# Half of a dense expert stage moved into a state-space recurrence, with B and C read from a ring of half-size tiles

## What is computed

```
h = adapter + layernorm(x)                       # per sequence, by language
for l in range(4):                               # the recurrence: 4 Mamba layers
    xz = norm(h) @ W_in;  u = silu(conv4(xs)+cb);  z = ...
    dt, B, C = split(u @ W_x);  dt = softplus(dt @ W_dt + b)
    for t: s = exp(dt*A)*s + dt*u*B ;  y = sum_states(s*C)      # 256 channels, 16 states
    h = h + ((y + u*Dp) * silu(z)) @ W_out
x1 = x + h
y = sum_e w_e * (silu(x1@Wg_e) * (x1@Wu_e)) @ Wd_e   # dense stage: 8 experts and a shared one, F = 512
out = x1 + top2_moe(y)                               # routing and sparse stage: 8 experts, gelu
```

## Time and profile before

| | |
|---|---|
| median of 3 runs | 2935.45 us (2935.06 to 2936.15) |
| profiled execution, its own time | 2935.85 us |
| its span, first to last instruction | 2934.1 us |
| VectorE busy / TensorE busy / GpSimd busy / ScalarE busy | 72% / 86% / 61% / 50% |
| mean granted TensorE clock | 0.946 |
| memory traffic | 354 MB, mean 121 GB/s |

### The profile page before, as it was taken

The page is one execution under the profiler, slowest core; times in us unless marked ns, Lnnn a source line. Parts: engine busy times, 40 slices in busy tenths (PEclk is TensorE's granted clock), DMA queues, the critical chain, the costliest instruction groups (busy, mean ns, idle before and its releaser), DMA issues. The chain is left out here.

```text
span 2934.1 us, 27727 instructions
## 1 busy us (share of the span) xinstructions
PE 2515.8 (86%) x6470; PEld 1112.9 (38%) x6470; DVE 2104.9 (72%) x2075; ACT 1456.5 (50%) x2337; POOL 1780.1 (61%) x1090
## 2 busy tenths in 40 slices
PE   5588888888888888888888888869999999999586
PEld 3233333333333333333333333324444444444264
DVE  4399999999999999999999999972333333333221
ACT  2366657666666665666566667632222222222222
POOL 3278887888888788888888887861022202221266
PEclk9798999999999999989999999999999999999798
DMA  7334533543453344345434533516000000000154
GB/s 204 139 128 179 201 127 144 194 170 127 170 197 139 136 185 186 127 157 196 154 128 174 205 127 142 195 61 220 8 15 8 15 7 11 25 8 1 45 111 70
DMA packets 130514, 354.33 MB, mean 121 GB/s; under 512 B 21716, under 2 KB 85410, under 8 KB 97570
## 3 DMA queue, kind: packets, MB, share of 16 engines
q1 hardware_dynamic: 116770, 342.46, 32.1%
q0 software_dynamic: 11264, 7.98, 1.8%
q10 hardware_dynamic: 2432, 3.38, 0.3%
HBM read 330.34 MB, written 23.99 MB: 121 GB/s over the span
## 5 line engine op out<-in xcount | busy, mean ns | idle before, releaser
L683 POOL TENSOR_TENSOR gg<-hh,Ct 128x1024 f32<-128x1024 f32 x512 | 1205.0, 2356 | 336.2 <-DVE hh L598 322.4
L598 DVE TENSOR_TENSOR_SCAN hh<-dA,psdB 128x1024 f32<-128x1024 f32 x512 | 1170.7, 2287 | 59.4 <-ACT dA L543 6.1
L385 PE MATMUL psY<-gg,ident 128*128 128x512 f32 x2048 | 1024.4, 636 | 128.0 <-POOL gg L683 127.7
L543 ACT ACTIVATE dA<-dt,Acur 128x508 f32<-128x508 f32 x1024 | 664.6, 707 | 14.9 <-DVE hh L598 14.4
L385 PEld LDWEIGHTS psY<-gg,ident 128*128 128x128 f32 x2048 | 390.9, 200 | 689.8 <-issue 420.6
L592 DVE TENSOR_TENSOR psdB<-psU,Bt 128x1024 f32<-128x1024 f32 x512 | 617.6, 1206 | 36.8 <-ACT psU L522 36.8
L1051 DVE TENSOR_TENSOR ac<-sg,d_bank 128x512 f32<-128x512 f32 x288 | 198.1, 688 | 514.0 <-PE d_bank L901 496.8
L948 ACT ACTIVATE sg<-d_bank 128x512 f32<-128x512 f32 x288 | 171.9, 597 | 534.6 <-PE d_bank L897 521.3
L811 POOL TENSOR_TENSOR xw<-x1T,wbc 128x512 f32<-128x512 f32 x72 | 74.9, 1041 | 568.1 <-PE d_bank L901 563.8
L897 PE MATMUL d_bank<-x1T,wgu 128*128 128x512 f32 x576 | 296.6, 597 | 1.9 <-DMA wgu<-in_Wu 1.9
L901 PE MATMUL d_bank<-xw,wgu 128*128 128x512 f32 x576 | 295.5, 595 | 0.0
(11 more groups left out here) (149 smaller groups left out, 1887.1 us busy)
## 6 DMA issues: line engine op xcount, KB each, us to landing
Bt<-rows SPq DMA_DIRECT2D x128, 1024.0 KB, 6.0
Ct<-rows SPq DMA_DIRECT2D x128, 1024.0 KB, 4.7
wcur<-taps_l SPq DMA_DIRECT2D x33, 512.0 KB
disp<-zrow SPq DMA_DIRECT2D x16, 528.0 KB, 12.1
dx<-disp SPq DMA_DIRECT2D x16, 528.0 KB, 6.5
wcur<-in_W_inT SPq DMA_DIRECT2D x33, 128.0 KB
diag<-diags_l SPq DMA_DIRECT2D x33, 128.0 KB
ad_gb<-in_gb SPq DMA_DIRECT2D x32, 128.0 KB, 3.3
```

The lines of the kernel that those rows point to most:

```text
L385: ins = pe.matmul(psY[:, :], lhsT=ident[:, :], rhs=gg[k % NGB][:, j, :], start=False, stop=(k % NK == NK - 1 and j == 1))
L543: ins = act.activation(dA[k % NDA][:, j, :, 1:T], dt[p][:, c, :, 1:T], ACT.Exp, scale=Acur[p][:, s:s + 1])
L598: dve.tensor_tensor_scan(out=hh[k % NHB][:, :, :].rearrange("p c t -> p (c t)"), data0=dA[k % NDA][:, :, :, :].rearrange("p c q t -> p (c ...
L683: pool.tensor_tensor(gg[k % NGB][:, :, :], hh[k % NHB][:, :, :], Ct[:, s:s + 2, :], ALU.mult).then_inc(prod, 1)
```

## The change

1. **Order of the recurrence.** The 32 iterations are 4 layers of groups 0 to 3, and after them 4 layers of groups 4 to 7 (`layer`, `group`; `ROUND` = 4). All is unrolled, no loop is left in the recurrence or the dense stage.
2. **Dense stage of groups 0 to 3 inside the second half** (iterations from `FIRST` = 15). Nine rounds per iteration are threaded through the steps by `G_AT`, `U_AT`, `D_AT`: gate, up and down products on TensorE, a copy of each gate out of PSUM (`place_gate`), one silu over the nine (`silu_gates`) beside the iteration's own, one product each on VectorE (`act_product`), the scaling on GpSimd (`scale`). Weights come from memory once for each group. The dense stage that follows has four groups.
3. **PSUM.** One of the two `psdB` tiles becomes the gate and up tiles, one of the two tiles for `dt*u` the down sum. So from iteration 13 (`RING0`) there is one `psdB` and one `psT`, filled for each channel half just before it (`turn0`, `turn1`).
4. **SBUF.** From iteration 13, B and C are rings of four pairs each; the second channel half takes the pairs backwards, 7 to 0. There are 12 loads of one pair of B and one of C for each iteration, 512 KB each.
5. **Steps by halves.** From iteration 15, in 8 of 16 steps (`PAIRED`) GpSimd adds the two halves of `gg`, and TensorE does one product instead of two.
6. **Given steps.** In iterations 0 to 12, GpSimd makes the input term of three steps (`GIVEN`) in SBUF, and ScalarE moves it into `psdB`.
7. The residual is added by one more identity product in the output projection, and no longer by GpSimd. The dispatch buffer is cleared during the recurrence. `x0` stands on TensorE ahead of the step 0 sums.

```diff
-NCK, CKS = 4, NS // 4
-WUSE = 9
-OUTP = 7
+ROUND = NG // 2
+NPR = NS // 4
...
+FIRST = NL * ROUND - 1
+RING0 = FIRST - 2
...
-ACT_AT = {1: ["params", "dtu1"], 2: ["norm"], 3: ["sums1"], 5: ["x0"], 6: ["x1"], 7: ["z0", "z1"], 8: ["silu"], 10: ["bcdt"], 11: ["dt0", "dt1"],
+ACT_AT = {1: ["params", "dtu1"], 2: ["turn0", "norm"], 3: ["sums1"], 5: ["x0"], 6: ["x1"], 7: ["z0", "z1"], 8: ["silu"], 10: ["turn1", "bcdt"], 11: ["dt0", "dt1"],
...
+GIVEN = {4: 0, 9: 5, 13: 8}
+POOL_AT = {3: ["gate1"], 6: ["rstd"], 10: ["dt"], 11: ["dtu"], 12: ["gate0"]}
+G_AT = [-9, -8, -6, -5, -4, -3, -2, -1, 3]
+U_AT = [6, 8, 9, 11, 12, 14, 15, 19, 20]
+D_AT = [10, 10, 11, 13, 14, 18, 18, 21, 22]
+T_AT = 5
+PAIRED = [0, 1, 2, 5, 8, 13, 14, 15]
...
+def pair(i, k):
+
+    return k if k < NK else (k - NK if i < RING0 else NSTEP - 1 - k)
...
+                    last = 1 if i >= FIRST and k in PAIRED else 2
+                    for j in range(last):
+                        ins = pe.matmul(psY[:, :], lhsT=ident[:, :], rhs=gg[k % NGB][:, j, :], start=False, stop=(k % NK == NK - 1 and j == last - 1))
...
+                def silu_gates(v):
+                    act.wait_ge(gfree, use_g(NB * v + NB - 1) + 1)
+                    lo = NB * v % NSLG
+                    for a, b in ((lo, min(lo + NB, NSLG)), (0, lo + NB - NSLG)):
+                        if b > a:
+                            ins = act.activation(sg[:, a:b, :], sg[:, a:b, :], ACT.Silu)
+                    ins.then_inc(sg_ok, 1)
...
+                    b, free = (k % NDB, n + 1 - NDB) if i < RING0 else (0, n)
+                    at_least(dve, scan, free)
...
+                    if i >= FIRST and k in PAIRED:
+                        ins.then_inc(half, 1)
+                        pool.wait_ge(half, len(PAIRED) * (i - FIRST) + PAIRED.index(k) + 1)
+                        ins = pool.tensor_tensor(gg[k % NGB][:, 0, :], gg[k % NGB][:, 0, :], gg[k % NGB][:, 1, :], ALU.add)
...
-                def body(g, p, prev, more):
+                residual(0)
+                for h in range(NDT):
```

More of the change, by code:

```diff
@@ L296, in mamba_phase @@
[L296 to L316, removed]
+        Bhi, Chi = (late[:, 2 * NPR * b:2 * NPR * (b + 1), :].rearrange("p (n s) t -> p n s t", s=2) for b in range(2))
@@ new lines, in wave_phase, with tile, arrived @@
+        b_ld, c_ld = ([sem(f"{n}_ld{j}") for j in range(NS // 2)] for n in "bc")
+        g_ld, ud_ld = ([sem(f"{n}_ld{j}") for j in range(NXW)] for n in ("fg", "fud"))
+        W = psw_uses()
+        plan = spreads()
+        loads = {}
+        for i, k, s, j, free in plan:
+            loads[i, k] = 16 * sum(1 for a, b, _, l, _ in plan if l == j and (a, b) <= (i, k))
+        def tile(lo, hi, j):
+            return lo[:, j, :, :] if j < NPR else hi[:, j - NPR, :, :]
+        def arrived(eng, ld, i, k):
+            if (i, k) in loads:
+                eng.wait_ge(ld[slot(i, pair(i, k))], loads[i, k])
@@ L349, in first @@
[L349 to L366, removed]
@@ L370, in _ @@
+                sp.wait_ge(zeroed, 16 * 2 * NE)
             @block.tensor
             def _(pe):
[L372 to L380, removed]
@@ new lines, in down @@
+                def down(n):
+                    e, f = expert(n)
+                    pe.wait_ge(acted, n + 1)
+                    if n % NST == 0:
+                        at_least(pe, sum_ok, n // NST)
+                    pe.matmul(psD[:, :], lhsT=fwd[:, e % NXW, f, :], rhs=sg[:, n % NSLG, :], start=(n % NST == 0), stop=(n % NST == NST - 1)).then_inc(downed, 1)
+                transposes(0)
+                for k in sorted(PE_AT):
+                    for what in PE_AT[k]:
+                        if what in PRE:
+                            pre(0, what)
@@ L692, in body @@
+                            if what == "rstd" and i + 2 < NIT:
                                 deviation(i + 2)
-                            if more and what == "dt":
-                                time_step(i + 1, 1 - p)
-                            if more and what == "dtu":
-                                time_input(i + 1, 1 - p)
-                loop(pool, body, first, lambda: gate(NIT - 1, 1, 1))
+                            if what == "dt" and i + 1 < NIT:
+                                time_step(i + 1)
@@ L701, in dense_phase @@
+                            if what == "dtu" and i + 1 < NIT:
+                                time_input(i + 1)
+                gate(NIT - 1, 1)
 def dense_phase(nc, A, K, out):
@@ L753, in at_least, with posts, sums @@
                 eng.wait_ge(sm, v)
-        def loop(eng, first, body, last):
-            first()
-            body(0, 0, False, True)
-            with eng.Fori(0, NG // 2 - 1) as j:
-                body(2 * j + 1, 1, True, True)
-                body(2 * j + 2, 0, True, True)
-            body(NG - 1, 1, True, False)
-            last(NG - 1, 1)
+        def posts(h, r, at):
+            return [2 * h + j for j in range(2) if 2 * h + j < NG - 1 and r == P_AT[j] + at]
+        def sums(g):
+            return h_res[:, G * g:G * (g + 1), :]
         with nc.Block() as block:
@@ L1249, in mega @@
             setup_phase(nc, A, K, M)
-            mamba_phase(nc, A, K, M)
+            wave_phase(nc, A, K, M, out)
         with ExitStack() as c5:
```

889 lines of the change are left out of this document (536 added, 353 removed).

## The result

| | before | after |
|---|---|---|
| median | 2935.26 us (2933.83 to 2936.15, 4 runs) | 2887.13 us (2885.38 to 2888.60, 4 runs) |
| ratio, with its 95% interval | | 0.9836 [0.9824, 0.9847] |
| span of the profiled execution | 2934.1 us | 2883.6 us |
| recurrence, first input term to end of last scan | 1842.2 us | 2165.8 us |
| last scan to last copy of a group's down sum | 776.2 us | 405.9 us |

The account below looks back on a forecast made before the run. It took VectorE to bound the recurrence and TensorE the dense stage, with a TensorE-ScalarE loop deciding later iterations: 2934.1 - 370 - 43 + 6 + 243 + 3 = 2773, forecast as 2774.5 us, range 2640 to 2870.

Parts of the forecast that it names:

- Dense stage, -370: Dense stage: four groups' products leave at 92.5 us each, the routing of all eight stays; -370 us.
- What decides from iteration 15 on: Iterations 15 to 30: a TensorE-ScalarE hand-off loop, above every engine's own load, sets the time; +243 us.
- rival 1: Second half: the hand-off loop is hidden and VectorE bounds, 64.3 to 69 us an iteration; 2642 us at 64.5; chance 0.21.
- Its size, 72.8: Iterations 15 to 30: loop parts 40.4 + 29.8 + 2.4, with a few semaphores, make 72.8 us an iteration.
- xd to sums0: the gate copied at step 12: +0.6: Loop stretch from xd to the end of sums0: ScalarE's added gate copy lengthens it by 0.6 us.
- The same at the same place costs half of 4.7: +2.4: Loop from skip of step 8: TensorE's slow products after its wait, before full pace returns, cost 2.4 us.
- Iterations 0 to 12, -43: First iterations with given steps: each falls from 57.6 to 54.3 us, -43 us; bounds -52 and 0.
- do not mesh perfectly: I take 54.3: Iterations 0 to 12: VectorE at 53.6 and GpSimd at 53.0, sharing four tiles, give 54.3 us an iteration.
- Rival 2: Iterations 0 to 12: the given steps do nothing and iterations stay at 57.6 us; 2817 us; chance 0.10.
- Iterations 13, 14, +6: With one psdB tile the input term waits for the scan: 0.18 us a step, 2.9 an iteration, +6 us.
- Rival 3: Second half: TensorE falls to its low clock, the kernel getting slower than before; 2970 us at clock 0.80; chance 0.06.
- Rival 4: Second half: the ring of B and C loads runs dry; losing 5 us an iteration gives 2855 us; chance 0.04.

Follow-up runs that it names:

- x1: Changed kernel with the silu of the expert gates cut to one column of each gate (leaves out work): 2826.48 us, ratio 0.9626.
- x3: Changed kernel with ScalarE copying the first-half sums ahead of the gate copy and softplus, in all iterations: 2815.37 us, ratio 0.9587.
- x6: Changed kernel with x3's order, xd and turn1 copied earlier from iteration 15, and dt0, dt1 copied earlier: 2790.77 us, ratio 0.9506.
- x2: Changed kernel with six zero products on TensorE where it waits, in 12 of the last 16 iterations: 2846.59 us, ratio 0.9694.
- x8: Changed kernel without the given steps (GIVEN = {}), VectorE making all input terms: 2911.55 us, ratio 0.9924.
- x9: x6 with the sums copied ahead of softplus only from iteration 15 on: 2774.97 us, ratio 0.9448.
- x10: x9 together with the zero products of x2: 2776.43 us, ratio 0.9458.
- x12: x9 with two zero products on TensorE ahead of dt1, in 12 of the later iterations: 2755.07 us, ratio 0.9388.
- x7: Changed kernel without expert work in the recurrence (NDF = 0), the dense stage having eight groups again: 2984.36 us, ratio 1.0170.

## Why the prediction was wrong

- *Dense stage, -370*: right (-373.7).
- *What decides from iteration 15 on*: right. The loop TensorE to ScalarE and back sets the time (x1, x3, x6), the waits named for steps 8 to 11 and ahead of dt0 and `skip` are the longest there, and rival 1 (VectorE's 64.3) is out: x1 cuts nothing on VectorE and gains 61 us.
- *Its size, 72.8*: here the forecast failed. The step is "xd to sums0: the gate copied at step 12: +0.6", together with "The same at the same place costs half of 4.7: +2.4". The first took the added copy by its own length and not by when its input arrives: it is behind dt1 and two sums on TensorE, and all of them run at the low clock. That clock was in the trace at this very place, at no cost, since nobody waited for the sums; the second step priced it behind `skip` only. Measured: +4.6 there. x3 takes the order away, with softplus, and gains 72 us; x2 takes half of the low clock (0.92 to 0.96) and gains 40. So the kind of loss is shown by runs; how the 4.6 divide (1.1, 2.9, 0.6) is read from the rows of one iteration. The rest is 1.0 up to z1 and 1.3 from `skip` to x0. 78.55 for 72.8 is 92 us of the 113 missed.
- *Iterations 0 to 12, -43*: too large, about -25. "... do not mesh perfectly: I take 54.3" was 55.2. The waits of the first half (150 to 863) have it: VectorE waits for ScalarE's move of the given term and for late decays.

```profile
DVE hh L811 <- ACT psdB L708: 17.7, 13, 1.4
...
DVE hh L811 <- ACT dA L717: 12.6, 13, 3.1
```

  The forecast asked whether GpSimd gives the time back. It is nearly full (623 of 654 us), but these two waits of VectorE are for ScalarE, whose place in order wasn't priced. No run takes them away, so that they are the missing 18 us is argued, not shown. Rival 2 is out: x8 is 24 us slower.
- *Iterations 13, 14, +6*: 60.2 and 63.2 for 60.5 each, 2 us more.
- *Rival 3*: the clock in the second half was 0.91, so it was not the 0.84 or less that makes the kernel slower, but the mechanism was in the result. It was kept as a case of its own with 6 in 100, and the likeliest case had only +2.4 of it, at one place of two.
- *Rival 4*: out. The table of waits has none for the ring.
- *The range*: its upper bound for the iteration, 80 (+358), held what came. Its end at 2870 did not: it took in only "some of rivals 3 and 4", and with 80 us an iteration the sum is 2774.5 + 16 x 7.2 = 2890.
- *Small slips of the sum*: GpSimd's terms add up to 59.3, not 59.5; 108 x 0.86 is 92.9, not 92.5; the silu over the gates in two pieces costs 2 x 0.60 + 7 x 0.46 = 4.4, not 4.3. None of them matters here. That x9 ends at 2774.97, the number that was forecast, is chance: it has 71.4 us an iteration for 72.8 and 55.2 for 54.3.

## What to carry to other kernels

Where an in-order engine gets one more copy, price it by when its input is ready, and then look at what stands behind it: here a copy of 0.6 us and the low clock around it cost 4.6, and one change of order on ScalarE was worth 72 us. A low clock that costs nothing today, because nobody waits for those products, is a price as soon as the change puts something behind them. Once a loop is shortened until an engine's own instructions are the bound, the same remedy stops working (x2 brought 40 us, in x10 nothing), so ask anew which wait ends last after each step.

## What the runs showed of the hardware that was not expected

- Products with zeros keep the granted clock up, for 0.86 us each. From 1080 to 2000 it is 0.96 in x2 for 0.92 without them, and 0.99 in x10 and in x12 for 0.95 in x9; x12 has two of them in 12 of the last 16 iterations, x10 six.
- The granted clock says little of the time by itself. From 1080 to 2000 x7 has 0.82 at 61.3 us an iteration, x10 0.99 at 71.7, and x10 is no faster than x9 with 0.95:

```profile
1080.00:2000.00 920.00, 726.21 (x1505) 284.02 (x1503) 860.36 (x599) 542.84 (x861) 835.80 (x473) 0.82 0.66 220
```

- Halving the loads did no harm: from 1080 to 2330 the 512 KB loads landed in 5.0 and 4.5 us at 193 GB/s, where before 1 MB of B took 6.0 and 1 MB of C 4.7, at 167. The DMA issues of this stretch after:

```profile
Blo<-rows SPq DMA_DIRECT2D x184, 512.0 KB, 5.0
Clo<-rows SPq DMA_DIRECT2D x184, 512.0 KB, 4.5
```

What stays open: by their number (72 x 0.86, and 0.6 for the transposes) TensorE's products and the zero ones are 62.5 of x12's 70 us; which of its remaining waits (for z1, for the adds, for `skip`) could still go was not tried, nor another choice of `PAIRED`.
